# One loop for the last 28 groups of two causal convolutions, with the tiles re-placed to allow it, on one Trainium2 core

## The reference, cut to what matters

```
k = u Wk' + bk,  v = u Wv' + bv,  q = u Wq' + bq        (per channel d: a sequence of 512)
k = causal_conv(k, k_kernel[d]) + k_D[d] * k             (512 taps, by FFT in the reference)
kv = k * v
y = (causal_conv(kv, ssm_kernel[d]) + D[d] * kv) * q
x = layernorm(u + y Wo' + bo)
```

## Time and profile before

| | us |
|---|---|
| median of three runs (lowest, highest) | 876.06 (873.8, 876.26) |
| the profiled execution | 876.8 |
| its span in the trace | 874.6 |
| PE busy in the span | 743.9 (85%) |
| DVE busy | 701.9 (80%) |
| ACT busy | 529.7 (61%) |
| POOL busy | 390.6 (45%) |

### The profile page before, as it was taken

How to read it: one execution, slowest core, us unless ns; L and a number is a source line. 1 busy time by engine, 2 the same in 40 slices (tenths; PEclk the granted TensorE clock), 3 DMA queues, 4 the chain that set the end, 5 groups by cost and what they waited for, 6 DMA issues and landing times.

```text
span 874.6 us, 26708 instructions
## 1 busy us (share of the span) xinstructions
PE 743.9 (85%) x11392; PEld 545.2 (62%) x11392; DVE 701.9 (80%) x1100; ACT 529.7 (61%) x625; POOL 390.6 (45%) x307
## 2 busy tenths in 40 slices
PE   0067979999999878775499999999999999999993
PEld 0067869999999878774355555555555555554541
DVE  6895637877777666777559999999999999999885
ACT  2383738887787767564364556665556655566661
POOL 0331213222322222221565668766678666687542
PEclk9998989999999999877699999999999999999996
DMA  9994759999999867684000110111100111101001
GB/s 335 341 240 127 181 131 214 221 227 224 222 219 226 195 156 152 149 198 134 25 25 1 48 49 0 48 48 48 48 28 20 48 48 48 48 0 49 25 25 48
DMA packets 55579, 101.01 MB, mean 115 GB/s; under 512 B 5728, under 2 KB 41440, under 8 KB 53600
## 3 DMA queue, kind: packets, MB, share of 16 engines
q1 hardware_dynamic: 54144, 97.94, 43.6%
q10 hardware_dynamic: 1376, 2.23, 0.7%
HBM read 89.92 MB, written 27.01 MB: 134 GB/s over the span
## 4 chain that ended last, share of the span: by engine, by line
PE 41%; DVE 29%; POOL 16%; issue 10%; ACT 2%; DMA 1%; SPq 0%; POOLq 0%; DVEq 0%; ACTq 0%
PE ps L741 15%; POOL arena L687 14%; PE ps L763 13%; DVE arena L1238 7%; PE ps L874 5%; PE ps L881 5%; DVE u_maxima L975 2%; DVE arena L1195 2%; DVE arena L1235 2%; DVE arena L1043 2%; DVE arena L1214 2%; DVE qy L1046 2%; PE ps L855 2%; DVE arena L1046 2%; DVE arena L1220 2%
## 5 line engine op out<-in xcount | busy, mean ns | idle before, releaser
L741 PE MATMUL ps<-arena 128*128 128x96 f16 x3072 | 143.8, 210 | 68.5 <-DVE arena L1028 51.1
L687 POOL TENSOR_TENSOR arena<-arena 128x512 f16<-128x512 f32 x128 | 178.6, 1427 | 14.9 <-ACT arena L570 14.3
L741 PEld LDWEIGHTS ps<-arena 128*128 128x128 f16 x3072 | 138.6, 101 | 71.9 <-issue 56.2
L881 PE MATMUL ps<-arena 128*128 128x512 f16 x768 | 173.2, 379 | 2.7 <-POOL arena L687 2.7
L874 PE MATMUL ps<-arena 128*128 128x512 f16 x768 | 170.8, 379 | 0.9 <-issue 0.9
L763 PE MATMUL ps<-arena 128*128 128x64 f16 (+2 forms) x5088 | 146.9, 183 | 27.1 <-issue 14.5
L763 PEld LDWEIGHTS ps<-arena 128*128 128x128 f16 x5088 | 143.5, 98 | 29.0 <-issue 21.4
L652 POOL TENSOR_TENSOR arena<-arena 128x512 f16<-128x512 f32 x32 | 37.2, 1162 | 247.5 <-ACT arena L526 247.5
L1227 DVE TENSOR_TENSOR arena<-arena 128x512 f32<-128x512 f32 x128 | 138.4, 1135 | 9.6 <-POOL arena L687 7.9
L566 ACT ACTIVATE arena<-ps,read_factor 128x512 f32<-128x512 f32 x128 | 88.0, 687 | 78.2 <-PE ps L874 61.4
L881 PEld LDWEIGHTS ps<-arena 128*128 128x128 f16 x768 | 73.9, 98 | 90.5 <-POOL arena L687 9.6
(11 more groups left out here) (108 smaller groups left out, 899.3 us busy)
## 6 DMA issues: line engine op xcount, KB each, us to landing
arena<-kpad_dram SPq DMA_DIRECT2D x166, 256.0 KB, 5.2
kpad_dram<-ksplit_dram SPq DMA_DIRECT2D x64, 256.0 KB, 6.0
qy<-in_uT SPq DMA_DIRECT2D x8, 1024.0 KB, 17.4
arena<-in_u SPq DMA_DIRECT2D x16, 512.0 KB, 4.1
out<-arena SPq DMA_DIRECT2D x16, 512.0 KB, 3.0
qy<-kpad_dram SPq DMA_DIRECT2D x22, 256.0 KB, 6.3
arena<-in_k SPq DMA_DIRECT2D x2, 512.0 KB, 4.8
ksplit_dram<-arena ACTq DMA_DIRECT2D x2, 512.0 KB, 3.7
```

The source lines that it names most:

```text
L687: nc.gpsimd.tensor_tensor(h16[:, 1, f], h_square[:, f % 4], h16[:, 0, f], ALU.subtract).then_inc(h_lo, 1)
L741: last = nc.tensor.matmul(o, u16[:, x, t, tok:tok + P], wcur[:, w, t], start=(k == 0), stop=(k == 3 * DT - 1))
L881: return nc.tensor.matmul(PD[:, t], wp16[:, w, f, t * P:(t + 1) * P], h16[:, h, f], start=first, stop=last)
```

## The change

Five things change together:

1. PE's code: steps 0 to 3 are written out, and steps 4 to 31 are one loop of 14 passes. Two outer `If`s leave the projection out from group 28 on; a further `If` in the second convolution of odd groups picks one of two places for half 0. After the loop only conv2(31) is left.
2. Places: an even group's tiles lie in BASE. An odd group's half 1 lies in a new place of its own, ODD (a seventh half tile in `T`), and its half 0 in QUERY (now the last chunk of `qy` only) up to group 23 and in TOKENS (the tokens of the first quarter, high part) from group 25. LATE and `T2` are gone, with two memsets and a wait on DVE.
3. To make room for ODD, `kbuf` shrinks from 16 KB to 8 KB: the keys of the next chunk are written over those of this one, quarter by quarter, in a transposed order, into the slice that group g has given free. DVE waits for `k_lo` of group g before it reads the projection out. For odd chunks the keys are written by four instructions of 128 elements instead of one of 512.
4. DVE's step reads the projection first and then does `times_v`.
5. The wait of the query part of `read_projection` for the last use of QUERY is there for the last chunk only (group 24), and conv1's copies are counted by a semaphore for each half. `wo`, `bo_b` and the staging of the second stage move in memory.

The diff, cut to its core:

```diff
-        kbuf = part(16, F32, "p (r q n) -> p r q n", r=2, q=GPC)
+        kbuf = part(8, F32, "p (a b n) -> p a b n", a=GPC, b=GPC)
...
-        T = part(6 * 8, F16, "p (k c a n) -> p k c a n", k=6, c=HG, a=2)
-        at[0] = 48 * KB
-        T2 = part(2 * 8, F16, "p (k c a n) -> p k c a n", k=2, c=HG, a=2)
-        T3 = qy[:, (NC - 2) * CH * COL:].bitcast(F16).rearrange("p (k c a n) -> p k c a n", k=2, c=HG, a=2)
-        T4 = u16[:, :, :, 0:TOK // GPC].rearrange("p k t (c n) -> p k t c n", n=L)
+        T = part(7 * 8, F16, "p (k c a n) -> p k c a n", k=7, c=HG, a=2)
+        T3 = qy[:, (NC - 1) * CH * COL:].bitcast(F16).rearrange("p (c a n) -> p c a n", c=HG, a=2)
+        T4 = u16[:, 0, :, 0:TOK // GPC].rearrange("p t (c n) -> p t c n", n=L)
...
         def keys_of(s):
-            n = s % GPC * (GC // GPC)
-            return kbuf[:, s % PAIR // GPC, :, n:n + GC // GPC].rearrange("p q (m b) -> p q m b", b=4)
+            nth = s % GPC
+            keys = kbuf[:, nth] if s % PAIR // GPC else kbuf[:, :, nth]
+            return keys.rearrange("p q (m b) -> p q m b", b=4)
...
-        BASE, LATE, QUERY, TOKENS = range(4)
-        QUERY_UNTIL = NG - 3 * GPC
-        TOKENS_FROM = NG - 2 * GPC
+        BASE, ODD, QUERY, TOKENS = range(4)
+        TOKENS_FROM = NG - 2 * GPC + 1
         def slot_of(g, half):
-            if g >= TOKENS_FROM:
-                return ((LATE if g >= NG - GPC else TOKENS, half) if g % 2 == 0 else (BASE, half))
-            if g < QUERY_UNTIL:
-                return (QUERY, half) if g % 2 else (BASE, half)
-            three = ((BASE, 0), (BASE, 1), (QUERY, 1))
-            return three[(2 * (g - QUERY_UNTIL) + half) % 3]
+            if g % 2 == 0:
+                return (BASE, half)
+            if half:
+                return (ODD, half)
+            return (TOKENS if g >= TOKENS_FROM else QUERY, half)
...
+            def conv2_half(s, g, half, place):
+                pe.wait_ge(c2_copied, 2 * g + half + 1)
+                windows = windows2_in(place, half)
+                convolve(half, PC2[:, s % 2], kv16[:, s % 2], lambda c, a: windows[:, c // 2, c % 2 * 2 + a], c2_half)
...
+            def pair_of_steps(nth):
+                g = FIRST + 2 * nth
+                with pe.If(nth < (NG - GPC - FIRST) // 2):
+                    with pe.If(nth % 2 == 0):
+                        pe.wait_ge(wcur_ready, nth + FIRST // 2 + 2)
+                        project(0, g + GPC)
+                    with pe.Else():
+                        project(2, g + GPC)
+                conv1(0, g)
+                conv2_inputs(g - 1)
+                with pe.If(nth < (TOKENS_FROM + 1 - FIRST) // 2):
+                    conv2_half(1, g - 1, 0, QUERY)
                 with pe.Else():
+                    conv2_half(1, g - 1, 0, TOKENS)
+                conv2_half(1, g - 1, 1, ODD)
+                with pe.If(nth < (NG - GPC - FIRST) // 2):
+                    with pe.If(nth % 2 == 0):
+                        project(1, g + 1 + GPC)
+                    with pe.Else():
+                        project(3, g + 1 + GPC)
+                conv1(1, g + 1)
+                conv2(0, g)
+
+            FIRST = GPC
+            for g in range(FIRST):
                 step(g)
+            with pe.Fori(0, (NG - FIRST) // 2) as nth:
+                pair_of_steps(nth)
             conv2(NG - 1, NG - 1)
...
+                if r == 0:
+                    nc.vector.scalar_tensor_tensor(kbuf[:, quarter].rearrange("p b (d m) -> p (b d) m", d=G),
+                                                   keys, read_factor[:, 0:1], bias_k, ALU.mult, ALU.add)
+                else:
+                    for n in range(GPC):
+                        some = slice(n * G, (n + 1) * G)
+                        nc.vector.scalar_tensor_tensor(kbuf[:, n, quarter].rearrange("p (d m) -> p d m", d=G),
+                                                       keys[:, some], read_factor[:, 0:1], bias_k[:, some],
+                                                       ALU.mult, ALU.add)
...
-                    if s == 2 and quarter == 0 and chunk >= NC - 2:
-                        g0, h0 = USES[QUERY, chunk - (NC - 2)][-1]
+                    if s == 2 and quarter == 0 and chunk == NC - 1:
+                        g0, h0 = USES[QUERY, 0][-1]
                         dve.wait_ge(c2_half, 2 * g0 + h0 + 1)
...
             def step(s, base, more, chunk, first=False):
                 g = base + s
-                times_v(s, g, base + (s // GPC + 1) * GPC)
                 if more:
+                    dve.wait_ge(k_lo, g + 1)
                     if s % GPC == 0 and not (first and s == 0):
                         dve.wait_ge(kv_lo, g)
                     read_projection(s % GPC, (s // GPC + 1) % 2, g + GPC, chunk + s // GPC + 1)
+                times_v(s, g, base + (s // GPC + 1) * GPC)
...
-                if s == GPC - 1:
-                    nc.vector.memset(T2[HP:P].rearrange("p k c a n -> p (k c a) n")[:, :, 0:HP], 0.0
-                                     ).then_inc(t_zero, 1)
-                    nc.vector.memset(T2[QP:HP].rearrange("p k c a n -> p (k c a) n")[:, :, 0:QP], 0.0
-                                     ).then_inc(t_zero, 1)
-                    dve.wait_ge(t_zero, 4)
```

More of the change, by code:

```diff
@@ L167, in build @@
         yT = part(4, F32, "p (t n) -> p t n", t=DT)
+        wo = part(2, F32, "p (t n) -> p t n", t=DT)
+        bo_b = part(1, F32)
         sum1 = part(4, F32, "p (i n) -> p i n", i=NI)
@@ L290, in windows1_of, with windows2_in @@
             return T[:, s % 2 * 2 + half]
-        def windows2_of(g, half):
[L293 to L297, removed]
+        def windows2_in(place, half):
+            if place == TOKENS:
+                return T4.rearrange("p t (c a) n -> p t (c a) n", a=2)
+            t = (T[:, 4 + half], T[:, 6], T3)[place]
+            return t.rearrange("p (t c) a n -> p t (c a) n", t=2)
+        def windows2_of(g, half):
+            return windows2_in(*slot_of(g, half))
         def shifted(windows):
@@ L406, in loaded_at @@
                     return max(g - 1, use_before(g, half)[0] + 1)
-                return 0 if slot_of(g, half)[0] == QUERY else TOKENS_FROM if slot_of(g, half)[0] == TOKENS else g - 1
+                return g - 1
             for s in range(NG):
@@ L417, in _ @@
                 for g, half in second:
-                    if not use_before(g, half) and slot_of(g, half)[0] != LATE:
+                    if not use_before(g, half):
                         load_windows2(g, half)
@@ L516, in copy_windows @@
                 act.wait_ge(c1_masked, 2 * g + half + 1)
-                nc.scalar.activation(*as_pairs(*shifted(windows1_of(s, half))), ACT.Copy).then_inc(c1_copied, 1)
+                nc.scalar.activation(*as_pairs(*shifted(windows1_of(s, half))), ACT.Copy).then_inc(c1_copied[half], 1)
             def copy_windows2(g, half):
@@ L745, in project, with convolve @@
                 last.then_inc(proj, 1)
[L747 to L768, removed]
+            def convolve(half, out, data, taps, done):
+                for c in range(HG):
+                    ch = half * HG + c
+                    k = 0
+                    for delta in range(NI):
+                        cols = (NI - delta) * B
+                        for tp, xp in ((0, 0), (0, 1), (1, 0)):
+                            last = nc.tensor.matmul(out[:, ch * COL + delta * B:(ch + 1) * COL],
+                                                    taps(c, tp)[:, delta * P:(delta + 1) * P],
+                                                    data[:, xp, ch * COL:ch * COL + cols],
+                                                    start=(k == 0), stop=(k == 3 * NI - 1))
+                            k += 1
+                last.then_inc(done, 1)
             pe.wait_ge(ld_wcur, 16)
@@ L790, in conv2 @@
                     pe.wait_ge(y_ready, g - 1)
-                convolve(1, PC2[:, s % 2], lambda a, ch: kv16[:, s % 2, a, ch * COL:(ch + 1) * COL],
-                         lambda half, c, a: windows2_of(s, half)[:, c // 2, c % 2 * 2 + a],
-                         g + 1, c2_half)
+            def conv2(s, g):
+                conv2_inputs(g)
+                for half in range(2):
+                    conv2_half(s, g, half, slot_of(s, half)[0])
             def step(g):
@@ L805, in step @@
                     conv2(g - 1, g - 1)
[L807 to L811, removed]
-                with pe.Else():
[L813 to L825, removed]
+            def pair_of_steps(nth):
[10 more added lines that the diff above has]
+                    conv2_half(1, g - 1, 0, QUERY)
+                with pe.Else():
+                    conv2_half(1, g - 1, 0, TOKENS)
[9 more added lines that the diff above has]
+            for g in range(FIRST):
                 step(g)
-            with pe.Fori(0, len(LOOPED) // 2) as nth:
-                pair_of_steps(LOOPED.start, nth)
-            for g in range(LOOPED.stop, NG):
-                step(g)
```

(22 more changed lines are left out.)

53 lines of the change are left out of this document (24 added, 29 removed).

## The result

The changed kernel takes **981.29 us** (median of 4 runs, 977.1 to 983.43) against 875.57 us before (4 runs, 873.8 to 876.26): a ratio of 1.1202, 95% interval 1.1166 to 1.1239. The forecast, 855.3 us and faster, was wrong. The time lies in the range only because rival A, 920 to 985 us, was in it.

A forecast was written before the change was run, and what follows sets the result against it. Bound by PE in the loop and by arrival of PE's code outside it; -14.9 - 2.6 - 2.7 + 4.1 - 4.7 = -20.8 from 876.8 gave 856.0, so 855.3 us at the median; own range 847 to 866, eight in ten 847 to 985.

The forecast's parts named there:

- rival A: Loop's end: ninth code block replaces the first, one or two blocks fetched again each jump back; 920 to 985 us.
- Rival B: Loop's end: the whole body is fetched again in every pass; about 1080 us, up to 1160.
- Groups 21 to 27: These groups move into the loop and take 65.4 instead of 80.37 us: -14.9 (bounds -13.7 and -16.0).
- Groups 6 to 20: Loop: reading the projection first removes PE's wait, 9.35 instead of 9.52 us a group: -2.6 (bounds 0 and -4.8).
- Group 0: PE's 2.70 us wait before the projection of group 1 goes, as the read comes first: -2.7 (bounds 0 and -2.7).
- Group 3 and first pass: Group 3 written out, 11.5 us, and a longer first pass, 31.0: +4.1 (bounds +2 and +6).
- Groups 28 to 31: Earlier key split and one code stop less before conv2(27) carry to the end: -4.7 (bounds -2 and -7).
- Second stage: The part after the first stage, taken as unchanged: 0.
- Rival C: Loop: later `times_v` makes conv1 wait for `k_lo`, 0.5 us in each of 24 groups: +12, 867 us.
- Rival D: Code stops stay or are replaced by stops at the branches, in about the same sum: 870 to 879 us.

The follow-up runs named there:

- after_pad30: Changed kernel with 30 matmuls (60 instructions) put in ahead of its loop, which then ends 75 instructions into the eighth block: 1100.8 us.
- after_pad76: Changed kernel with 76 matmuls (152 instructions) put in ahead of its loop, which then ends in the seventh block: 864.81 us, ratio 0.9882 to the kernel before.
- before_readfirst: Kernel before, unpadded, with only DVE's new order, the read of the projection before `times_v`: 869.49 us, ratio 0.9932.
- pad76_last: Changed kernel with 76 matmuls of padding and, in group 27 alone, `times_v` before the read: 861.02 us, and 858.85 us in a second set of runs.
- before_pad88: Kernel before with 88 matmuls (176 instructions) put in ahead of its loop, which then ends 19 instructions into the eighth block: 936.25 us, ratio 1.0722.
- after_pad16: Changed kernel with 16 matmuls (32 instructions) put in ahead of its loop, which then ends 47 instructions into the eighth block: 1003.8 us.

## Why the prediction was wrong

**The step that failed** is the weighing of the forecast against rivals A and B: "I hold eight blocks to be enough slightly likelier than not". By it the sum put the loading of code in the later passes at nothing, and the runs show six reloads of nine blocks, 19.4 us each, 116.5 us together. The arithmetic ahead of it was right to a few instructions (835 pairs of body; 833 in the program; 10 pairs into the eighth block; 15 instructions). The trace had shown that eight blocks are held, seven of the loop and the next, and this is what holds. Where the body reaches the eighth, all of it is loaded again. That the ninth block takes the place of the first, and each block loaded anew that of the next one needed, is how I read the nine packets; no run shows the places. The Trainium skill, Runtime: NRT & Kernel Launch, section Instruction fetch mechanics, says 2048 instructions for PE, that is eight blocks, and the runs agree with it to 5 instructions on one side and 15 on the other. That count, and that each fetch ahead had been seen to happen, should have made the rivals the forecast. What I set against them, that such a fetch would be poor design, came from no row.

**Rival A** gave the right size, 920 to 985 us, by a wrong mechanism: one or two blocks at each of 13 jumps. **Rival B** had the right mechanism, the whole body, but at each jump. What runs is B at every second jump: nine blocks, six times, 19.4 us each. B proper was 1080, up to 1160, and is after_pad30, 1100.8 us. (The upper bound was summed wrongly: 13 passes at 8 x 5.1 instead of 18.7 us give 1142.)

**The terms of the sum**, with the loop where it fits (trace of after_pad76 against that of before, both in single executions):
- Groups 21 to 27: -14.9 forecast, 66.29 for 80.37, **-14.1**. The main reason of the change was right. The wait in group 24 and the DMAs of TOKENS cost nothing that shows.
- Groups 6 to 20: -2.6 forecast, 141.47 for 142.80, **-1.3**. It is two terms: the order gives -0.27 a group (forecast with the branches -0.17), the branches take 0.2. They were bounded, 0 to 0.19 each, and taken too low. DMA, which I had late next at 9.3 us, does not bind: the old loop runs at 9.25.
- Group 0: -2.7 forecast, **0**. The projection of group 1 does start 3.0 us earlier, at 80.19. Then PE waits 1.33 for POOL and, at two block starts, 1.11 and 2.03, and group 3 starts at 104.51 in both kernels. Unpadded, the changed kernel starts it at 102.43 and then stops 2.24 us for code in it. In before_readfirst, with other block starts, it keeps 1.8.
- Group 3 and first pass: +4.1 forecast, 40.97 for 38.44, **+2.5**. The pass took 30.57 (31.0 forecast), group 3 only 10.40 (11.5).
- Groups 28 to 31: -4.7 forecast, 43.73 for 44.78, **-1.0**. I had followed `times_v(27)` as if it kept its place. It moves behind the read, and there PE has no projection to cover it. Put back (pad76_last), it returns 1.6 of the missing 3.7. Even then PE waits 3.04 us, where 1.5 was forecast, and its next 192 matmuls take 6.94 us at a granted clock of 0.55, where 5.16 was the value at full clock.
- Second stage: 0 forecast, +2.1 in this pair. It is not traced to anything: from its first copy to the end it takes 462.5 to 465.0 us over all the traces here, 462.9 in the kernel before, and 464.3 and 462.6 in two traces of one kernel, pad76_last.

Sum -11.8 where -20.8 was forecast; the spans differ by 874.6 - 862.8 = 11.8.

**Rival C** (another chain the bound) holds only at single groups: PE waits 1.33 us for POOL's low part of the keys at group 1, and 4.86 behind group 27. **Rival D** (stops at the branches) is there with 0.42 to 0.51 us a pass.

**Left open:** which jumps reload when the body ends 15 to 47 instructions into the eighth block. In the changed kernel the pass that had itself loaded the eighth block never did, and the next one always did; but the second pass of before_pad88 loaded nothing and did not reload at its end either, and in after_pad16 the first jump reloads (PE stands 10.25 us) though the first pass had loaded the eighth block. So neither is a rule, and what makes the difference was not tried.

The version that beats both kernels is the changed one, with its loop moved into seven blocks and `times_v` first in group 27: 858.9 and 861.0 us, 1.8% under the kernel before.

## What to carry to other kernels

Count PE's instructions, two for each matmul, up to the loop and through it, and take the place of the block starts from the stops marked "issue" in the trace. In these runs a loop can touch seven blocks of 256, and is reloaded where it touches eight. Padding ahead of it in PE's idle time cost nothing (the changed kernel's loop starts at 114.90 us without and 114.91 with 76 matmuls of it); a change anywhere earlier in PE's code can push it over, as 176 instructions did to the kernel before. And where a step is moved in a steady loop, read it once more for the last group, where the work that covered it is missing.

## What the runs showed that was not expected

- One reload costs 17 to 20 us for a body of 18.9 us a pass: not only the blocks' arrival, but a clock that falls meanwhile. In pass 3 the stops add up to 14.2 us, and its two projections take 3.5 us more together than twice 4.25.
- A loop just over the edge reloads in about every second pass, further over in every pass.
- While GpSimd subtracts, DVE's copies slow down, and GpSimd with them: line 1105 took 4.14 us for two copies where it takes 2.22 alone, and line 645 took 2.17 instead of 1.3. In pad76_last the overlap is shorter, and two copies take 3.18 us. It is seen in these two timelines; no run isolates it.
